# Row statistics one batch ahead, an earlier read-out of the last context, and earlier reciprocals in an attention and mixture-of-experts kernel

## The reference

```
xn  = layernorm(x)
s   = attention(xn)      # 16 heads of 32, ALiBi bias, causal softmax, output product + bias
g   = silu(ffn(xn))      # 2 experts, hidden 2048, each row goes to the expert with the larger logit
out = x + s * g
```

## Time and profile before

| what | value |
|---|---|
| runs of the kernel before | 1479.88, 1480.56, 1480.98 us, median 1480.56 us |
| the profiled execution | 1481.51 us, of which the span from first to last instruction is 1479.7 us |
| PE busy | 1384.0 us, 94% of the span |
| DVE busy | 923.9 us, 62% |
| ACT busy | 770.7 us, 52% |
| POOL busy | 682.5 us, 46% |
| mean granted TensorE clock | 0.987 of full speed |

### The profile page before, as it was taken

How to read it: one execution, slowest core, us unless ns; L and a number is a source line. 1 busy time by engine, 2 the same in 40 slices (tenths; PEclk the granted TensorE clock), 3 DMA queues, 4 the chain that set the end, 5 groups by cost and what they waited for, 6 DMA issues and landing times.

```text
span 1479.7 us, 30039 instructions
## 1 busy us (share of the span) xinstructions
PE 1384.0 (94%) x9863; PEld 880.8 (60%) x9863; DVE 923.9 (62%) x2441; ACT 770.7 (52%) x1824; POOL 682.5 (46%) x896
## 2 busy tenths in 40 slices
PE   2889999999999999999689999999999999999995
PEld 1455555655555565555456666666666666666663
DVE  7577777777777777777759745555444555544444
ACT  3478778787777878787736422222222222222221
POOL 0356667465666746566523433333333333323332
PEclk9989999999999999999999999999999999999998
DMA  4425334343534434245346311110011111010100
GB/s 161 144 86 148 125 115 125 110 139 100 171 101 130 128 106 138 89 141 140 107 164 207 115 44 44 44 43 25 23 41 42 39 44 44 30 29 30 36 30 30
DMA packets 84897, 133.45 MB, mean 90 GB/s; under 512 B 14095, under 2 KB 63247, under 8 KB 82576
## 3 DMA queue, kind: packets, MB, share of 16 engines
q1 hardware_dynamic: 75808, 105.70, 23.0%
q0 software_dynamic: 8944, 25.83, 5.6%
HBM read 97.81 MB, written 33.95 MB: 89 GB/s over the span
## 4 chain that ended last, share of the span: by engine, by line
PE 75%; DVE 10%; POOL 6%; ACT 3%; issue 3%; DMA 1%; DVEq 1%; SPq 0%; ACTq 0%; POOLq 0%
PE psY L1126 19%; PE psF L1106 19%; PE psA L352 19%; PE psT L446 7%; PE psA L461 5%; POOL pr L941 4%; PE psS L425 3%; DVE sg L1303 2%; PE psX L1080 1%; POOL route L969 1%; PE psA L409 1%; DVE stat L749 1%; DVE am L636 1%; ACT stage L519 1%; DVE wf L1225 1%
## 5 line engine op out<-in xcount | busy, mean ns | idle before, releaser
L1106 PE MATMUL psF<-xT,wf 128*128 128x256 f16 (+1 forms) x3264 | 368.0, 269 | 0.0
L1126 PE MATMUL psY<-wf,aT 128*128 x1584 | 363.9, 379 | 0.3 <-DVE aT L1270 0.3
L1106 PEld LDWEIGHTS psF<-xT,wf 128*128 x3264 | 312.0, 98 | 63.5
L1344 POOL TENSOR_TENSOR a<-a 128x512 f32<-128x512 f32 (+1 forms) x136 | 153.1, 1126 | 392.1 <-DVE a L1261 390.5
L941 POOL TENSOR_SCALAR pr<-pr,rden 128x128 f32<-128x128 f32 (+3 forms) x512 | 268.4, 542 | 141.9 <-DVE rden L868 140.3
L579 ACT ACTIVATE pr<-pr,mn 128x128 f32<-128x128 f32 (+3 forms) x512 | 281.9, 553 | 0.0
L857 DVE CUSTOM_DVE_ANT_0 pr<-psS,base,nsl 128x128 f32<-128x128 f32 (+3 forms) x512 | 249.6, 543 | 4.2 <-PE psS L425 4.2
L1126 PEld LDWEIGHTS psY<-wf,aT 128*128 128x128 f16 x1584 | 154.5, 98 | 158.5 <-issue 1.0
L446 PE MATMUL psT<-conf,pr 128*128 128x128 f32 x1280 | 205.7, 279 | 18.1 <-POOL pr L941 16.5
L1183 ACT ACTIVATE rl<-psF 128x512 f32<-128x512 f32 (+1 forms) x136 | 79.3, 583 | 263.2 <-PE psF L1106 263.0
L446 PEld LDWEIGHTS psT<-conf,pr 128*128 128x128 f32 x1280 | 157.3, 143 | 81.3 <-POOL pr L941 27.3
(11 more groups left out here) (155 smaller groups left out, 1371.0 us busy)
## 6 DMA issues: line engine op xcount, KB each, us to landing
qk_parts<-pre SPq DMA_DIRECT2D x64, 256.0 KB, 2.8
qs<-qk_parts SPq DMA_DIRECT2D x128, 128.0 KB, 2.7
ks<-qk_parts SPq DMA_DIRECT2D x128, 128.0 KB, 2.7
wst<-in_wf SPq DMA_DIRECT2D x16, 1024.0 KB
wstage<-in_wf SPq DMA_DIRECT2D x32, 512.0 KB, 4.6
xin<-in_x SPq DMA_DIRECT2D x32, 256.0 KB, 4.4
attn_out<-so SPq DMA_DIRECT2D x32, 256.0 KB, 2.0
pt<-in_wqkv SPq DMA_DIRECT2D x4, 768.0 KB, 10.1
```

Source lines behind the costliest of these rows:

```text
L1106: last = nc.tensor.matmul(psF[c % 2][:, k * TT:k * TT + tn], w(e, 2 * hc, hl, kc * 512 + col, P), xT[:, r % 2, x, kc, 0:tn], start=(m == 0 ...
L1126: last = nc.tensor.matmul(psY[r % 2][h][:], aT[:, c % 4, x, k, h * P:(h + 1) * P], w(e, 2 * hc + 1, hl, q * 512, 512), start=(c == 0 and k ...
L1344: nc.gpsimd.tensor_tensor(at, at, at, ALU.mult).then_inc(s["a_ready"], 1)
```

## The change

Three things are moved and two cut into parts; nothing is computed differently.

1. Row statistics of batch b+2 are made in steps 9 and 11 of iteration b (before: of batch b+1 in steps 0 and 1), with `mv` doubled. POOL's veps and rstd go from step 1 to step 12, and the loads of x move behind `stack(b, 3)` in SP's order.
2. The reciprocals of head s+2 are made in step s behind the copy of T2 and ahead of the step's extras (before: of head s+1 at the start of step s). So they now stand in the same step as the exponentials they need.
3. The last context: its DVE cast goes from step 2 to step 1, POOL's low half ahead of the q and k work of step 2, and in iteration 8 ACT and DVE do the splits of weight pieces 2 to 5 behind it. `weight_scales` goes from step 14 to step 15, behind `norm`, and the second PE transpose of the first slot goes behind the last context's product.
4. `choose` is cut: the logits are read in step 9, two instructions follow in step 10, the rest in step 11. `place` is cut: the rank is read in step 13, one half follows behind the reciprocals of step 13, the other in step 14. The scatters go to steps 4 to 7 of the next iteration (4 and 5 in the last).

```diff
+STATS_AT = {9: (0, 1), 11: (2, 3)}
...
-                rb, rh = head_at(b, step + N_LEAD)
-                if within(rb, 0, B):
-
-                    wait(dve, s["exp_done"], (rb * H + rh + 1) * QB)
-                    wait(dve, s["norm_done"], (rb * H + rh - HG + 1) * QB)
-                    c = (rh % HG) * QB
-                    nc.vector.reciprocal(rden[:, c:c + QB], den[:, c:c + QB]).then_inc(s["rden_done"], 1)
                 masked(0)
...
                 turned(2)
-                if more:
-                    if step < 2:
-                        ln_stats(2 * step)
-                        ln_stats(2 * step + 1)
-                    elif step < 6:
-                        ln_apply(step - 2)
+                rb, rh = head_at(b, step + E_LEAD)
+                if within(rb, 0, B):
+
+                    wait(dve, s["exp_done"], (rb * H + rh + 1) * QB)
+                    wait(dve, s["norm_done"], (rb * H + rh - HG + 1) * QB)
+                    c = (rh % HG) * QB
+                    nc.vector.reciprocal(rden[:, c:c + QB], den[:, c:c + QB]).then_inc(s["rden_done"], 1)
+                if b == -1 and step < 2:
+                    ln_stats(0, 2 * step)
+                    ln_stats(0, 2 * step + 1)
+                if more and 2 <= step < 6:
+                    ln_apply(step - 2)
+                if within(b, -1, B - 2):
+                    for i in STATS_AT.get(step, ()):
+                        ln_stats(b + 2, i)
+                if more and step in (10, 11):
+                    choose_rest(step - 10)
+                if more and step in (13, 14):
+                    place_rest(step - 13)
...
-                if j == (3 if g else 2):
+                if j == (3 if g else 1):
...
-                if b == B - 1 and step == 14:
-                    weight_scales()
                 if b == B - 1 and step == 15:
                     ffn["norm"](dve, 0, 1, 0)
+                    weight_scales()
                     ffn["split_lo"](dve, range(0, 2))
                 if b == B and step == 0:
-                    ffn["split_lo"](dve, range(2, 4))
-                if b == B and step in (1, 3):
-                    ffn["turn_lo"](dve, 0, step // 2, 0)
-                    ffn["split_lo"](dve, range(4 + step // 2, 5 + step // 2))
+                    ffn["turn_lo"](dve, 0, 0, 0)
+                if b == B and step == 3:
+                    ffn["turn_lo"](dve, 0, 1, 0)
+                    ffn["split_lo"](dve, range(2, 6))
```

On ACT, POOL, PE and SP:

```diff
-                if (b, step) in ((B - 1, 15), (B, 0)):
-                    ffn["split_hi"](act, range(2 * (step == 0), 2 * (step == 0) + 2))
-                if b == B and step in (0, 2):
-                    ffn["turn_hi"](act, 0, step // 2, 0)
-                    ffn["split_hi"](act, range(4 + step // 2, 5 + step // 2))
+                if (b, step) == (B - 1, 15):
+                    ffn["split_hi"](act, range(0, 2))
+                if b == B and step < 2:
+                    ffn["turn_hi"](act, 0, step, 0)
+                if (b, step) == (B, 1):
+                    ffn["split_hi"](act, range(2, 6))
...
+                if step == 2:
+                    ctx_low(b - 1, NG - 1)
...
-                if more and step == 1:
...
+                if b == -1 and step == 1:
+                    deviations(0)
+                if within(b, -1, B - 2) and step == 12:
+                    deviations(b + 2)
+                if g and j == 3:
+                    ctx_low(b, g - 1)
...
-                if more and step in (14, 15):
...
+                if within(b, 0, B) and 4 <= step < (6 if b == B - 1 else 8):
...
-                if b == B - 1 and step >= 14:
-                    ffn["xtrans"](pe, 0, step - 14)
+                if (b, step) in ((B - 1, 14), (B, 0)):
+                    ffn["xtrans"](pe, 0, int(b == B))
...
-            if within(b, 0, B - 1):
-                for i in range(QB):
...
+            if within(b, -1, B - 2):
+                for i in range(QB):
+
+                    wait(sp, s["xn_ready"], (b + 1) * QB + i + 1)
```

More of the change, by code:

```diff
@@ L491, in iteration @@
                     nc.tensor.transpose(psA[0][0:2, 0:P], fam[:, 0:2], conf[:, C_ID:C_ID + P]).then_inc(s["fam_turned"], 1)
-                if b == B - 1 and step == 13:
+                if b == B - 1 and step == 14:
                     pe.wait_ge(s["fam_row"], 1)
@@ L738, in iteration, with ln_stats @@
             more = within(b, -1, B - 1)
[L739 removed]
             def link(ins):
[L743 removed]
+                n_link[0] += 1
                 ins.then_inc(s["dve_link"], 1)
[L745 to L748 removed]
+                dve.wait_ge(s["dve_link"], n_link[0])
+            def ln_stats(batch, i):
+                wait(dve, x_in[i], (batch + 1) * 16)
                 link(nc.vector.bn_stats(stat[:, i, :], xin[:, i, :]))
[L750 removed]
+                nc.vector.bn_aggr(mv[:, batch % 2, i, :], stat[:, i, :]).then_inc(s["ln_stats"], 1)
             def ln_apply(i):
@@ L924, in att_gpsimd, with ctx_low, deviations @@
     def att_gpsimd(pool, ffn):
+        def ctx_low(batch, group):
+            if within(batch, 0, B):
+                pool.wait_ge(s["ctx_hi"], batch * NG + group + 1)
+                nc.gpsimd.tensor_tensor(cx[:, group, 1, :], cf[:], cx[:, group, 0, :], ALU.subtract
+                                        ).then_inc(s["ctx_lo"], 1)
+        def deviations(batch):
+            pool.wait_ge(s["ln_stats"], (batch + 1) * QB)
+            wait(pool, s["meta_ready"], batch - 1)
+            nc.gpsimd.tensor_scalar(veps[:], mv[:, batch % 2, :, 1], 1e-5, 1.0, ALU.add, ALU.mult
+                                    ).then_inc(s["pool_link"], 1)
+            pool.wait_ge(s["pool_link"], batch + 1)
+            nc.gpsimd.tensor_tensor(rstd[:, batch % 2, :], veps[:], half[:], ALU.pow
+                                    ).then_inc(s["rstd_ready"], 1)
         def iteration(b, odd):
@@ L948, in iteration @@
                                             ALU.subtract).then_inc(s["qk_lo"], 1)
-                if more and step == 1:
-                    wait(pool, s["ln_stats"], (nxt + 1) * QB, s["apart_pool"])
-                    wait(pool, s["meta_ready"], nxt - 1, s["apart_pool"])
-                    nc.gpsimd.tensor_scalar(veps[:], mv[:, :, 1], 1e-5, 1.0, ALU.add, ALU.mult
-                                            ).then_inc(s["pool_link"], 1)
-                    wait(pool, s["pool_link"], nxt + 1, s["apart_pool"])
-                    nc.gpsimd.tensor_tensor(rstd[:, par, :], veps[:], half[:], ALU.pow
-                                            ).then_inc(s["rstd_ready"], 1)
-                pb, pg = (b, g - 1) if g else (b - 1, NG - 1)
-                if j == (3 if g else 2) and within(pb, 0, B):
-                    wait(pool, s["ctx_hi"], pb * NG + pg + 1, s["apart_pool"])
-                    nc.gpsimd.tensor_tensor(cx[:, pg, 1, :], cf[:], cx[:, pg, 0, :], ALU.subtract
-                                            ).then_inc(s["ctx_lo"], 1)
+                if b == -1 and step == 1:
[4 more added lines that the diff above has]
+                    ctx_low(b, g - 1)
                 if b == B - 1 and step in (10, 12):
                     ffn["gather_x"](pool, 0, 0, (step // 2 - 5,))
-                if more and step in (14, 15):
-                    wait(pool, s["meta_ready"], nxt + 1, s["apart_pool"])
-                    for i in (2 * step - 28, 2 * step - 27):
+                if within(b, 0, B) and 4 <= step < (6 if b == B - 1 else 8):
+                    pool.wait_ge(s["meta_ready"], b + 1)
+                    for i in ((2 * step - 8, 2 * step - 7) if b == B - 1 else (step - 4,)):
                         nc.gpsimd.indirect_dma_start(
```

70 lines of the change are left out of this document (37 added, 33 removed).

## The result

The changed kernel takes **1491.03 us** (median of four runs, 1490.79 to 1495.49) beside 1480.22 us for the kernel before (four runs, 1479.54 to 1480.98): a ratio of 1.0078, 95% interval 1.0061 to 1.0095. It is slower: small, but clear of the noise. The profiled execution took 1491.05 us with a span of 1489.2 us, against 1479.7 us: +9.5. The forecast was 1487.5 us, range 1479 to 1496.

A forecast was written before the change was run, and what follows sets the result against it. PE was taken to set the pace, busy 82.23 of 85.47 us a batch. Terms -13.5 + 4.2 + 12.4 - 1.3 - 1.0 + 6.1 gave +6.9 us; from the 1480.56 median, 1487.5 us, range 1479 to 1496.

The forecast's parts named there:

- step 12 gap (head 13): PE waits 2.0 us at step 12's scores in six batches, +12.0, and +0.4 in batch 6 for `choose`.
- step 15 gap (head 0): Routing in parts delays step 15's masked scores: new gap 0.87 us, seven times, +6.1.
- last batch, up to head 4 or 5: PE's 1.1 us wait before T0 of head 4 goes, with its delayed scores: -1.3 us.
- slip: Last batch: weight maximum now runs behind DVE's wait for ACT, 1.3 us in step 9, 0.9 in step 11, 2.2 in all.
- behind head 15, to the "o" products: Last context of the last batch comes sooner: -3.2 us; with the slip, "o" products start at 742.0 against 743.0.
- Part 1a: Statistics leave steps 0 and 1: 2.0 of the 2.66 us before head 3 stays won a batch, sum -13.5.
- Part 1b: Statistics in steps 9 and 11 make new gaps of 0.70 us at step 10 and 2.0 at step 12 a batch.
- rival (a): Added DVE work hides in DVE's waits, so parts 1b and 4 cost nothing: 1455.6 us, chance 0.12.
- the profile's five signs: After the change: head-3 wait gone, norm waits near 1 us, masked waits about 30, period near 87, "o" waits under 6.
- Part 4: Routing in parts: step 13 comes out level, step 15 gets a new gap of 0.87 us, seven times, +6.1.
- Rival (c): PE's clock falls to 1.2 GHz behind the new gap of step 12 in six batches: +10.8 us, 1498.3 us, chance 0.10.
- Rival (b): Both sides cancel, statistics' gain full at -17.9 and the tail at -3.3: +0.2 us, 1480.8 us, chance 0.20.

The follow-up runs named there:

- experiment 2: Changed kernel with the statistics pairs in steps 8 and 12 in place of 9 and 11: 1479.93 us, ratio 0.9991.
- experiment 8: Changed kernel with an extra pair of statistics, read by nothing, at the end of step 11: 1508.74 us, ratio 1.019.
- experiment 6: Changed kernel with the weight maximum ahead of the next head's reciprocals in the last batch only: 1489.8 us, ratio 1.0066.
- experiment 4: Changed kernel with the reciprocals back at the start of the next step, for head s+1: 1487.53 us, ratio 1.0039.
- experiment 5: Kernel before with the edits of the last context alone: 1475.58 us, ratio 0.9965.
- experiment 3: Changed kernel with `choose` and `place` whole again, in steps 9 and 13, scatters left as changed: 1475.31 us, ratio 0.9958.
- the repeat: Changed kernel as it is, measured once more at another time: 1494.48 us, ratio 1.0097.
- experiment 1: Changed kernel with row statistics and veps/rstd put back in steps 0 and 1: 1502.53 us, ratio 1.0138.
- experiment 7: Changed kernel with an extra pair of statistics, read by nothing, at the end of step 8: 1497.31 us, ratio 1.0115.
- experiment 11: Changed kernel with statistics in steps 8 and 12, routing whole, and the weight maximum ahead of the reciprocals in the last batch: 1463.49 us, ratio 0.9889.

## Why the prediction came out as it did

The forecast's mechanism was right, and most of its terms are too; the size was not: +7.3 us over the kernel before were forecast and +10.8 measured. By the starts of T0 (batch by batch) and of the first "o" product:

| term | forecast | measured |
|---|---|---|
| statistics out of steps 0 and 1 (heads 3 and 4) | -13.5 | -13.7, and -1.9 in small steps elsewhere |
| step 10 gap (head 11) | +4.2 | +4.1 |
| step 12 gap (head 13) | +12.4 | +12.6, with batch 6 +1.06 in place of +0.4 |
| half of `place` in step 13 (head 15) | 0 | +2.0 |
| step 15 gap (head 0) | +6.1 | +5.3 |
| last batch, up to head 4 or 5 | -1.3 | -0.5 |
| last batch, steps 9 to 15 (slip) | +2.2 | +3.8 |
| behind head 15, to the "o" products | -3.2 | -1.7 |
| sum | +6.9 | +10.0 (span +9.5) |

Two of these rows were not forecast at all and cancel by luck: -1.9 us in small steps (net of a first T0 that starts 0.36 later) and +2.0 at head 15. What is left of the difference is the last batch with its end, 3.8 us more than forecast, less 0.8 at head 0. The range was also narrower than its own bounds: added one by one, they give from about -10.6 to +17.4 us, 1470 to 1498 us, and not 1483.5 to 1494.

**Right.** Part 1a: the two ends were 2.66 and 1.5 and the value taken was 2.0; each batch keeps 1.95. The casts do meet POOL: 1.15 us for the context's. Part 1b: 0.70 and 2.0 against 0.69 and 1.90, from the duration of a pair and of `choose` and the point from which DVE's tail can begin. That DVE cannot begin earlier was the argument against rival (a); experiments 2 and 8 show from both sides, by taking a pair out of this tail and by adding one, that work in it is paid for. Four of the profile's five signs came: no wait before head 3, masked waits of 28.6 us for about 30, a period of 86.86 for 87, "o" waiting 5.3 us. The fifth did not: PE's waits for POOL's norm are 4.1 us in all and not near 1, and the last batch makes them.

**Wrong in size: the tail.** The forecast had -2.3 us for the last batch with its end, measured are +1.5. The term that failed is the slip: 1.3 us in step 9 and 0.9 in step 11, sized by the 1.05 us for which DVE waits in the earlier trace rows. In the changed kernel DVE waits 2.05 and 1.73 us for ACT there, and PE waits for POOL's norm as well (3.18 us before head 13). Experiment 6 shows that the maximum behind the reciprocals is 1.1 us of this. In experiment 4, with the reciprocals at the start, none of the slip is there up to head 14, so it comes with their place; how the rest of it splits is not settled by a run. The gain behind head 15 was 1.7 us where experiment 5, without the slip, has 2.4 and the forecast had 3.2; and the 1.1 us that went before head 4 of the last batch brought 0.5 and not 1.3, as the steps of T0 there are +0.9 at head 3, -1.8 at head 4 and +0.5 at head 5.

**Wrong in size: step 13.** Part 4 says that step 13 comes out level. It costs 0.29 in each batch, 2.0 in all: half of `place` now stands behind the reciprocals, which wait 0.60 us for ACT, and no longer directly behind the read of the rank. It also takes 1.5 us in place of 0.93 (experiment 3), as two of its instructions stand beside POOL's norm:

```profile
402.52 0.18 DVE L886 RECIPROCAL rden<-den 128x4 f32<-128x4 f32 x1 [0.60 <-ACT pr L580]
...
402.79 2.05 POOL L973 TENSOR_SCALAR pr<-pr,rden 128x128 f32<-128x128 f32 x4 [3.54 <-DVE rden L886]
402.84 0.17 DVE L822 TENSOR_SCALAR t<-tid 128x4 f32<-128x4 f32 x1
...
403.24 0.39 DVE L824 TENSOR_TENSOR t<-t 128x4 f32<-128x4 f32 x1
...
403.66 0.54 DVE L825 CAST pos<-t 128x4 int32<-128x4 f32 x1
```

**Rival (c) was no rival but a term.** Chance 0.10 was given to a clock that falls behind the new gap in every batch. It falls in some batches of some executions: none in the first profile, two in the repeat, three in experiment 4, four in experiment 6, five in experiment 1, each with 1.4 to 1.7 us. The argument against it (the clock stays full behind the 2.66 us of step 2) is true of the kernel before and did not carry over. By the Trainium skill's TensorE: Matmul & The Clock Gate (Part 1) an idle TensorE is taken back to 1.2 GHz; the trace agrees in kind, with 0.58 granted behind gaps of 1.14 and 0.33 us, and also shows the same gaps with 1.00. A forecast of such a kernel needs some us for it on the slow side. Rival (b) needed the whole 2.66 us at heads 3 and 4 and a gain of 3.3 us from the slip and the last context together; measured are 1.95 and a loss of 2.0 (+3.8 and -1.7).

## What to carry to other kernels

A busy share of 62% says little about where an engine has room. Find for each step the last wait of the helping engine, and the first thing behind it that the bound engine needs: work put ahead of that wait is free as far as the wait is long (experiments 2 and 7), work behind it is paid in full once the slack there is gone (experiment 8). When a stall is removed, look at what stands next in the same queue, because two edits can be worth something only together, and try each part of a change of many parts alone: here one part (the tail) won 5 us, one (the routing in parts) lost 15, and the whole looked like a small loss.

## What the runs showed of the hardware that was not expected

**DVE instructions that wait out a POOL instruction.** In batch 6 the first instruction of the second part of `choose`, on 4 numbers a row, took 0.90 us, against 0.14 in other batches:

```profile
649.11 1.16 POOL L981 TENSOR_TENSOR pre<-stage,pre 128x512 f16<-128x512 f32 x1 [1.03 <-DVE pre L783]
...
649.39 0.90 DVE L800 TENSOR_SCALAR ef<-dl 128x4 f32<-128x4 f32 x1
```

It ended at 650.29, POOL's instruction at 650.27; the copy of experiment 6 ended at 732.94 and POOL's norm at 732.90. Both are SBUF to SBUF. At 389.30 the statistics took their usual 0.66 us beside a POOL instruction of 1.16 us, and copies out of PSUM their usual 0.42. So it depends on the DVE instruction, but its kind alone doesn't decide: another TENSOR_SCALAR on 4 numbers took 0.17 us at 402.84 (shown with step 13), with 0.32 us left of the first of the four POOL instructions in that row. What separates the two was not found. The price is what is left of POOL's instruction (0.90 us above), and in experiments 6 and 11 of all four instructions of a norm, up to 1.7 us for a copy of 0.14. The Trainium skill's GPSIMD Engine Reference (Specifications) names the shared SBUF interface and DVE's two-port modes; it gives no size, and these rows do.

**The clock.** Behind the same waits of the same program PE was granted 1.00 in one execution and 0.58 in another, and each such stretch cost 1.4 to 1.7 us. No run here shows what decides it.
